# A graph layer in one launch: y rows read into three buffers, the end stage's first weights multiplied later, the first sums fetched at another place, and another order on VectorE in stage two

## Chip, cores and metric

The kernel is one program on one core of one Trainium2 chip. The metric is the device time of one execution in microseconds (us), lower is better, given as the median of several executions. Five engines run their own instruction lists: TensorE (PE in the profile, PEld for its weight loads), VectorE (DVE), ScalarE (ACT), GpSimd (POOL) and SyncE (SP). They meet only through semaphores that the program sets and waits for by hand.

## The reference, cut to what matters

All on 6250 rows of 512 numbers, in float32:

```python
xn = layernorm(x)                                    # 6250 x 512
h  = relu(xn @ W1 + b1) @ W2 + b2                    # a small network for each row
gnn = h + segment_sum(h[dst], src, 6250)             # 100000 edges: rows of h added up
k, q, v = split(layernorm(xn, g1, c1) @ kqv_w + kqv_b)
kp, qp = exp(k @ w.T - |k|^2/2) / 16, exp(q @ w.T - |q|^2/2) / 16
y = v + ((qp @ (v.T @ kp).T) / (qp @ sum(kp))) @ proj_w + proj_b
mix = y + gelu(layernorm(y, g2, c2) @ mlp_w1 + b) @ mlp_w2 + b2
x1 = x + gnn + mix
out = x1 + haar_ffn(layernorm(x1))                   # fc1, gelu and fc2 on the low-pass half
```

The fc1 of the last line acts on an interpolated row. The kernel folds the interpolation matrix and fc1 into one small matrix on the chip ("the end stage's first weights": `interp` times `fc1_t`).

## The kernel before, in words

The 6250 rows are 125 partitions times 50 tiles, and each of the 25 steps of a stage takes two tiles (250 rows, 500 KB). There are five stretches.

1. The start and **stage one** (up to about 450 us): weights are folded, keys and the hidden rows of the edge network are made, and the edges are sorted on VectorE.
2. **The turn** (to 512 us): small matrices between the stages.
3. **Stage two**, 25 turns (`phase2`, 512 to about 1026 us): TensorE makes v and the y product of step u and the q products of step u+1. The transposed x rows (`x_t`) come by DMA into `xt`, ScalarE copies their high halves (`high_parts`, L1300) and VectorE makes the low halves (`low_parts`, L1621); both halves are operands of step u+2. VectorE also squares (`square_sums`, L1745), makes exponents (`kqw_rows`, L1737), writes y rows (L2010), takes their statistics (`row_stats`, L1891) and so lets `store_y` write them to HBM.
4. **The mlp stage**, 25 turns (about 1026 to 1480 us). y rows and x rows come back by DMA: `load_yd` (L491) and `load_xd` (L513). ScalarE normalises y (`norm_rows`, L1397), TensorE transposes it (`transposes`, L980), makes the first layer (`features`, L1075 to L1077) and the second (`mlp2`, L1086 to L1088). VectorE adds x and y (`skip_rows`, L2051 and L2053) and then the second layer (`z_rows`, L2074), and SyncE stores z (`store_z`, L548). x and z share three buffers `z3`: x of step u+3 can be loaded only when z of step u has landed (`z_stored`). y rows have two buffers `y3`.
5. **The end stage** (to 1750 us): for the steps in another order, sums of the edges (`ACC`, fetched with `fetch_sums`, L529, transposed at L1110) meet z, and the fc1 and fc2 products follow.

From the turn on, all engines also work off 440 **groups** of edges: GpSimd gathers rows, ScalarE makes one-hot matrices (L1372, L1376: `one_hots`, four groups in a batch, made ahead by `hits_until`), TensorE multiplies (L942 to L945) into one of two banks, and VectorE adds the bank to `ACC` (L1871, `add_groups`). TensorE may be two groups ahead of VectorE's adds. How many groups stand at each place of a turn is fixed by the tables `SECOND`, `MLP` and `LAST`.

The order of everything on an engine is the order in which the program is written. All DMAs but the gathers are issued by SyncE, in its own order, on one queue. SyncE waits for each semaphore before it goes on, and an issue also waits while the queue is full. The part of SyncE's list between stage two and the mlp stage is, before the change:

```python
            sp.wait_ge(v_mm, STEPS + 1)
            load_yd(0, 1)
            load_xd(0)
            sp.dma_start(mlp2_w, chunks(d["L0_mix_mlp_w2"])).then_inc(w2m_in, 16)
            load_xd(1)
            load_xd(2)
            store_y(Step(2, STEPS - 1))
            sp.dma_start(gnn2_w, chunks(d["L0_gnn_W2"])).then_inc(late_in, 16)
            ...
            sp.dma_start(fc1_t, chunks(d["fc1_t"])).then_inc(ev_fc, 16)
            for a in range(STEPS):
```

and `late_io(a)` in the loop issues the loads and stores of turn a. "x of step u" and "y(u)" below are the 500 KB of that step. TensorE's order in mlp turn a is: features of step a, first half; groups; transposes of step a+1; mlp2 of step a-1, in two halves with groups between; features, second half; groups.

## Time and profile before

| | us |
|---|---|
| median of 3 runs | 1753.76 |
| lowest and highest run | 1750.54, 1756.96 |
| the profiled execution, own time | 1752.63 |
| its span in the profile | 1750.1 |
| TensorE busy | 1549.2 (89%) |
| GpSimd, VectorE, ScalarE busy | 1002.2, 1134.8, 820.4 |
| mean granted TensorE clock | 0.958 |

The span is the time from the first to the last instruction; 2.5 us of the execution's own time lie around it. A busy share says how full an engine is, not whether it is waited for; for that, one reads the idle pieces of the fullest engine, and what ended each. The granted clock is a share of TensorE's full 2.4 GHz; 0.50 is its other level, 1.2 GHz.

### The profile page before, as it was taken

Reading aid. Unit: us, or ns where it says so; the run is one execution under the profiler, and the core shown is the slowest. Engines: PE = TensorE matmul, PEld = TensorE weight load, DVE = VectorE, ACT = ScalarE, POOL = GpSimd, SP = SyncE. Lnnn points to the kernel's source line nnn. Section 1 sums busy time; section 2 is a strip of 40 time slices with the busy share of each in tenths; the row PEclk is TensorE's granted clock in tenths of the full one; section 3 lists DMA queues with packets and bytes.
Section 4 is the critical chain, followed back from the end, with each engine's and each line's share of the span. In section 5 each row is a group of like instructions: output and inputs, shape, how many; then the busy total and the mean of one; then the engine's idle time right before and its main releaser. Section 6 shows DMA issues by size and latency. Waiting matters only on the chain.

```text
span 1750.1 us, 26882 instructions
## 1 busy us (share of the span) xinstructions
PE 1549.2 (89%) x8883; PEld 1249.3 (71%) x8883; DVE 1134.8 (65%) x2523; ACT 820.4 (47%) x1896; POOL 1002.2 (57%) x1057
## 2 busy tenths in 40 slices
PE   5999999898888999998999976989898896689996
PEld 3778877787667778877778755877777775366664
DVE  6899999998245566545655553655565563478885
ACT  2235445454365434434534464566466462355552
POOL 3023443343677767775677776777777773456610
PEclk8999999999899999998999987999999998799997
DMA  6023222222345555655556565555555553566642
GB/s 195 13 78 122 86 92 89 89 89 72 119 121 166 185 159 168 180 171 152 169 168 185 160 195 165 196 189 191 189 194 189 193 182 108 154 206 211 204 161 73
DMA packets 88682, 263.63 MB, mean 151 GB/s; under 512 B 18555, under 2 KB 20603, under 8 KB 88546
## 3 DMA queue, kind: packets, MB, share of 16 engines
q1 hardware_dynamic: 47490, 149.05, 25.2%
q0 software_dynamic: 41056, 112.88, 22.3%
q8 instruction: 72, 1.18, 0.3%
q14 instruction: 64, 0.52, 0.1%
HBM read 210.64 MB, written 44.90 MB: 146 GB/s over the span
## 4 chain that ended last, share of the span: by engine, by line
PE 38%; DMA 24%; DVE 19%; ACT 7%; issue 6%; POOL 3%; SPq 2%; DVEq 1%; POOLq 0%; ACTq 0%
DVE sb_weights L1564 6%; DMA z_rows<-sb_step 5%; DMA sb_step<-x_t 4%; PE bank L1029 4%; DMA sb_step<-x 4%; DMA sb_step<-sb_acc 4%; PE bank L992 3%; PE bank L994 3%; PE bank L993 3%; DMA z_rows<-sb_weights 2%; ACT sb_weights L1372 2%; DMA sb_step<-y_rows 2%; DMA sb_weights<-x 2%; DVE sb_step L1745 2%; PE bank L943 1%
## 5 line engine op out<-in xcount | busy, mean ns | idle before, releaser
L679 POOL DMA_INDIRECT sb_weights<-hidden_rows,sb_weights x830 | 829.2, 999 | 366.5 <-issue 224.4
L1372 ACT ACTIVATE sb_weights<-sb_const,sb_weights 128x125 f16<-128x125 f16 x880 | 266.3, 389 | 41.4 <-PE turn_bank L945 41.4
L1871 DVE TENSOR_TENSOR sb_acc<-sb_acc,bank 125x257 f32 x220 | 92.4, 420 | 159.9 <-PE bank L945 144.3
L1871 DVE TENSOR_TENSOR sb_acc<-sb_acc,turn_bank 125x257 f32 x220 | 92.1, 419 | 120.7 <-PE turn_bank L945 110.9
L1564 DVE TENSOR_TENSOR sb_weights<-sb_weights 128x512 f32<-128x512 f32 (+3 forms) x256 | 164.4, 684 | 3.6
L1290 ACT ACTIVATE sb_step<-sb_step 125x256 f32<-125x256 f32 x100 | 48.9, 504 | 211.8 <-DVE sb_step L1737 211.1
L646 POOL TENSOR_SCALAR sb_const<-sb_const 125x2 f32<-125x2 f32 x25 | 10.1, 403 | 239.6 <-ACT sb_step L1274 239.6
L784 PE MATMUL bank<-sb_w_parts,sb_x_high 128*125 128x512 f32 (+1 forms) x400 | 140.0, 350 | 0.0
L785 PE MATMUL bank<-sb_w_parts,sb_x_high 128*125 128x512 f32 (+1 forms) x400 | 135.8, 339 | 0.0
L786 PE MATMUL bank<-sb_w_parts,sb_x_low 128*125 128x512 f32 (+1 forms) x400 | 135.7, 339 | 0.0
L1376 ACT ACTIVATE sb_weights<-sb_weights,sb_const 128x1000 f16<-128x1000 f16 x110 | 124.2, 1129 | 3.6
L1397 ACT ACTIVATE sb_step<-sb_step,sb_const 125x512 f32<-125x512 f32 x50 | 37.9, 805 | 175.6 <-DMA sb_step<-y_rows 173.7
L797 PE MATMUL bank<-sb_w_parts,sb_x_high 128*125 128x256 f32 (+1 forms) x300 | 102.9, 343 | 15.6 <-DVE sb_step L1745 12.9
L1411 ACT COPY sb_step<-bank 128x500 f32<-128x500 f32 x25 | 14.4, 577 | 210.1 <-PE bank L1014 210.1
L799 PE MATMUL bank<-sb_w_parts,sb_x_low 128*125 128x256 f32 (+1 forms) x300 | 94.8, 316 | 0.0
L798 PE MATMUL bank<-sb_w_parts,sb_x_high 128*125 128x256 f32 (+1 forms) x300 | 94.7, 316 | 0.0
L2065 DVE CAST sb_gelus_high<-sb_step 128x500 fp32r<-128x500 f32 x50 | 21.5, 429 | 112.9 <-ACT sb_step L1428 112.8
L1029 PE MATMUL bank<-sb_const,sb_step 128*125 128x512 f32 x200 | 93.9, 591 | 0.0
L897 PE MATMUL bank<-sb_step 125*128 125x256 f32 x400 | 90.8, 380 | 1.1 <-ACT sb_step L1350 1.1
L942 PE MATMUL bank<-sb_weights 128*125 128x257 f16 x220 | 62.2, 283 | 27.7 <-DVE sb_acc L1871 15.0
L1086 PE MATMUL bank<-sb_mlp_high,sb_gelus_high 128*125 128x512 f32 x200 | 85.0, 425 | 0.4 <-issue 0.4
L897 PEld LDWEIGHTS bank<-sb_step 125*128 125x128 f32 x400 | 75.3, 190 | 13.6 <-issue 2.9
(367 smaller groups left out, 4337.9 us busy)
## 6 DMA issues: line engine op xcount, KB each, us to landing
sb_step<-x SPq DMA_DIRECT2D x55, 500.0 KB
sb_step<-x_t SPq DMA_DIRECT2D x50, 500.0 KB, 6.1
sb_weights<-hidden_rows,sb_weights POOLq DMA_INDIRECT x830, 4.4
y_rows<-sb_step SPq DMA_DIRECT2D x25, 500.0 KB
sb_step<-y_rows SPq DMA_DIRECT2D x25, 500.0 KB
sb_weights<-x SPq DMA_DIRECT2D x20, 500.0 KB
z_rows<-sb_step SPq DMA_DIRECT2D x17, 500.0 KB
sb_step<-z_rows SPq DMA_DIRECT2D x13, 504.0 KB
```

Source lines behind the costliest of these rows:

```text
L679: pool.indirect_dma_start(out=ring[:, r % RING * 2 + h, 0:HID], out_offset=None, in_=table, in_offset=bass.IndirectOffsetOnAxis(ap=row_of[ ...
L784: pe.matmul(bk, high, rhs(0, c), start=c == 0, stop=False)
L785: pe.matmul(bk, high, rhs(1, c), start=False, stop=False)
L786: mm = pe.matmul(bk, low, rhs(0, c), start=False, stop=c == KC - 1)
L797: pe.matmul(outs[c], high, first, start=c == 0, stop=False)
L799: mm = pe.matmul(outs[c], low, first, start=False, stop=c == KC - 1)
L897: mm = pe.matmul((BC, BD)[k // 2][:, (k % 2) * M:(k % 2 + 1) * M], x_in[0:P, t.b, m, k * 128:(k + 1) * 128], kpn[0:P, m, :], start=False, ...
L1029: mm = pe.matmul(banks[m][0:P, :], qpT[:, c, m * P:(m + 1) * P], pmat[:, c, :], start=False, stop=c == KH - 1)
L1372: mm = act.activation(hit[q % 2][:, i, :], iota_h[:, :], ACT.Abs, bias=less_lane[:, q * BP + i // 2, i % 2:i % 2 + 1])
L1376: act.activation(hit[q % 2], hit[q % 2], ACT.Relu, scale=-1.0, bias=one_c[:, 0:1]).then_inc(hits, 1)
L1564: sort_op(dve.tensor_tensor(half(target, c, lo), a, b, op))
L1871: dve.tensor_tensor(dst, dst, (BE, BH)[n % 2][0:P, 0:RW], ALU.add).then_inc(g_add, 1)
```

## The change

Five edits, all in the order of work and in where rows lie; no arithmetic is added or removed.

- **y rows in three buffers.** `y3` gets a third place (`z_first[1]`), step u uses place u mod 3, and `late_io(a)` loads y(a+3) where it loaded y(a+2). y(0) is loaded in turn 23 of stage two (was: turn 11), and y(2) goes into the queue behind the `mlp2_w` load.
- **The end stage's first weights.** `fc1_t` gets a place in `mlp1_w`, is loaded in stage two's turn 12 (was: last of the loads between the stages), and `tail_weights` runs in mlp turn 2 (was: end of turn 0), in bank BB, with ScalarE's copy of its result moved along.
- **First sums.** The two `fetch_sums` move from turn 24 to turn 23, ahead of the store of z(22).
- **VectorE in stage two.** `low_parts(u+2)` moves from ahead of the squares of step u+1 to behind the y rows of step u. Squares and exponents are taken apart, with groups between.
- **VectorE in mlp turn 0.** `skip_rows(0)` moves behind `split_mlp2`.

```diff
-        y3 = [halves[1].rearrange("p (a b) -> p a b", b=D), y3_odd]
+        y3 = [halves[1].rearrange("p (a b) -> p a b", b=D), y3_odd, z_first[1]]
...
-        interp, fc1_t = (z4[h].rearrange("p a (b c) -> p (a b) c", c=HL) for h in (0, 1))
+        interp, fc1_t = (v.rearrange("p a (b c) -> p (a b) c", c=HL) for v in (z4[0], mlp1_w[:, 2:4, :]))
...
+            def load_yd(u):
+                sp.wait_ge(y_st[u % 2], 16 * (u // 2 + 1) + 1)
+                sp.dma_start(y3[u % 3][0:P], rows(y_d)[:, 2 * u:2 * u + 2, :]).then_inc(y_ld[u % 3], 16)
...
+                if t.u == STEPS - 2:
+                    sp.wait_ge(*made("mlp1_split"))
+                    load_yd(0)
...
-                elif t.u == 11:
-                    sp.wait_ge(r_st[0], 16 * 13 + 1)
-                    sp.wait_ge(r_st[1], 16 * 12 + 1)
+                elif t.u == 12:
                     sp.wait_ge(*made("mlp1_split"))
-                    load_yd(0, 0)
+                    sp.dma_start(fc1_t, chunks(d["fc1_t"])).then_inc(ev_fc, 16)
...
             def late_io(a):
-                if a + 2 < STEPS:
+                if a + 3 < STEPS:
                     sp.wait_ge(zadd, a + 2)
                     sp.wait_ge(h_rows, a + 2)
-                    load_yd(steps[a + 2].j, steps[a + 2].s)
+                    load_yd(a + 3)
                 if 2 <= a and a + 1 < STEPS:
                     z_stored(steps[a - 2])
                     load_xd(a + 1)
+                if a == STEPS - 2:
+                    fetch_sums(steps[0])
+                    fetch_sums(steps[1])
                 if a > 0:
                     store_z(steps[a - 1])
...
             sp.dma_start(mlp2_w, chunks(d["L0_mix_mlp_w2"])).then_inc(w2m_in, 16)
+            load_yd(2)
             load_xd(1)
...
-            sp.dma_start(fc1_t, chunks(d["fc1_t"])).then_inc(ev_fc, 16)
...
             def tail_weights():
 
                 pe.wait_ge(ev_fc, 33)
+                pe.wait_ge(feat_c, 2 * TAIL_TURN + 1)
...
-                        pe.wait_ge(ev("a_fc1"), 1)
                     pe.wait_ge(z_ok, a)
                     mlp2(steps[a - 1], 0)
+                if a == TAIL_TURN:
+                    tail_weights()
                 groups(counts[1])
...
-                add_groups(counts[0] + counts[1])
-                add_groups(counts[2] + counts[3] + counts[4])
-                if more:
-                    low_parts(Step(2, t.u + 2))
+                add_groups(counts[0] + counts[1] + counts[2] + counts[3])
                 if not last:
-                    q_rows(next_step(t))
+                    q_squares(next_step(t), 0)
+                add_groups(counts[4])
+                if not last:
+                    q_squares(next_step(t), 1)
                 add_groups(counts[5])
+                if not last:
+                    q_exponents(next_step(t))
...
                     add_groups(counts[6 + m])
+                if more:
+                    low_parts(Step(2, t.u + 2))
                 dve.wait_ge(y_read, t.u * 2 + 3)
...
+                if a > 0:
+                    skip_rows(steps[a])
...
                 if a == 0:
                     split_mlp2()
-                add_groups(counts[2])
+                    skip_rows(steps[a])
```

SyncE's list at the border of stage two and the mlp stage, after the last stores of y. L487 stores y, L491 loads y, L513 (L514 in the changed kernel) loads x, and `fc_t` at L581 is `fc1_t`. Before:

```order
L487 DMA y_rows<-sb_step 125x1024 x2
L491 DMA sb_step<-y_rows 125x1024
L513 DMA sb_step<-x 125x1024
L573 DMA sb_weights<-L_mix_mlp_w 128x4x512
L513 DMA sb_step<-x 125x1024
L513 DMA sb_weights<-x 125x1024
L487 DMA y_rows<-sb_step 125x1024
L577 DMA sb_weights<-L_gnn_W 128x2x512
L579 DMA sb_step<-fc_t 128x2x256
L580 DMA sb_weights<-c_interp 128x4x256
L581 DMA sb_weights<-fc_t 128x4x256
```

and now:

```order
L491 DMA sb_step<-y_rows 125x1024
L514 DMA sb_step<-x 125x1024
L577 DMA sb_weights<-L_mix_mlp_w 128x4x512
L491 DMA sb_weights<-y_rows 125x1024
L514 DMA sb_step<-x 125x1024
L514 DMA sb_weights<-x 125x1024
L487 DMA y_rows<-sb_step 125x1024
L582 DMA sb_weights<-L_gnn_W 128x2x512
L584 DMA sb_step<-fc_t 128x2x256
L585 DMA sb_weights<-c_interp 128x4x256
L491 DMA sb_step<-y_rows 125x1024 x2
```

The second y load (y(2)) now stands fourth, the last weight load is gone, and the two y loads at the end are y(3) and y(4), where y(2) and y(3) stood.

VectorE in the later part of a stage-two turn. L1621 makes the low halves of x_t for step u+2, L1745 squares, L1737 exponents, L1871 a group's add, L2010 a y row. Before, with the rows' numbers:

```order
1247 L1621 TENSOR_TENSOR sb_x_low<-sb_step,sb_x_high 128x1000
1248 L1745 SCALAR_TENSOR_TENSOR sb_step<-bank,sb_weights 125x512
1249 L1737 SCALAR_TENSOR_TENSOR sb_step<-bank,sb_const 125x256
1250 L1745 SCALAR_TENSOR_TENSOR sb_step<-turn_bank,sb_weights 125x512
1251 L1737 SCALAR_TENSOR_TENSOR sb_step<-bank,sb_const 125x256
1252 L1871 ISA
1253 L1871 TENSOR_TENSOR sb_acc<-sb_acc,turn_bank 125x257
1254 L2010 SCALAR_TENSOR_TENSOR sb_step<-bank,sb_const 125x512
```

and now, where the same instructions have lines L1624, L1748, L1740, L1874 and L2019:

```order
1227 L1748 SCALAR_TENSOR_TENSOR sb_step<-turn_bank,sb_weights 125x512
1228 L1874 ISA
1229 L1874 TENSOR_TENSOR sb_acc<-sb_acc,turn_bank 125x257
1230 L1740 SCALAR_TENSOR_TENSOR sb_step<-bank,sb_const 125x256 x2
1231 L2019 SCALAR_TENSOR_TENSOR sb_step<-bank,sb_const 125x512
1232 L1874 ISA
1233 L1874 TENSOR_TENSOR sb_acc<-sb_acc,bank 125x257
1234 L2019 SCALAR_TENSOR_TENSOR sb_step<-bank,sb_const 125x512
1235 L1874 ISA
1236 L1874 TENSOR_TENSOR sb_acc<-sb_acc,turn_bank 125x257
1237 L1624 TENSOR_TENSOR sb_x_low<-sb_step,sb_x_high 128x1000
```

The low halves have gone from ahead of the squares to behind both y rows; the statistics of the y rows, after which they are stored, come next.

TensorE where the end stage's first weights stood, at the end of mlp turn 0, before:

```order
L945 MATMUL turn_bank<-sb_weights 125x257
L1096 MATMUL bank<-sb_weights 128x256 x6
L1075 MATMUL bank<-sb_weights 128x250
L1076 MATMUL bank<-sb_weights 128x250
L1077 MATMUL bank<-sb_weights,sb_const 128x250
```

and now, in mlp turn 2 behind the first half of mlp2:

```order
L981 MATMUL turn_bank<-sb_const,sb_step 128x125 x4
L1087 MATMUL bank<-sb_mlp_high,sb_gelus_high 125x512
L1088 MATMUL bank<-sb_w_parts,sb_gelus_high 125x512
L1089 MATMUL bank<-sb_mlp_high,sb_gelus_low 125x512
...
L1098 MATMUL bank<-sb_step,sb_weights 128x256 x6
L943 MATMUL turn_bank<-sb_weights 125x257
```

The six products have moved over two turns, from ahead of step 1's features to behind the transposes of step 3 (L981) and half of mlp2 (L1087 to L1089).

## Rows read from the trace of the kernel before

**Rows 1.** Windows by stretch: us, busy of PE, PEld, DVE, ACT, POOL, PEclk, DMA share, GB/s.

```profile
512.00:1017.00 505.00, 483.48 (x2836) 391.48 (x2836) 285.79 (x797) 222.59 (x516) 355.00 (x359) 0.98 0.56 168
1017.00:1075.00 58.00, 29.69 (x192) 23.49 (x191) 19.12 (x37) 25.04 (x54) 43.16 (x43) 0.76 0.69 204
1075.00:1440.00 365.00, 332.24 (x2320) 280.34 (x2320) 212.37 (x366) 217.55 (x496) 266.39 (x267) 0.99 0.55 188
1440.00:1520.00 80.00, 50.26 (x251) 37.08 (x252) 25.10 (x56) 23.50 (x56) 32.98 (x35) 0.79 0.46 136
```

**Rows 2.** Waits of TensorE, whole span: us in total, times, longest.

```profile
PE bank L980 <- ACT sb_step L1397: 23.8, 20, 2.2
...
PE bank L1096 <- DMA sb_weights<-fc_t: 18.7, 1, 18.7
```

**Rows 3.** Stage two: waits of TensorE, then its timeline (start, us, work [idle before, releaser]).

```profile
PE turn_bank L942 <- DVE sb_acc L1871: 11.4, 4, 7.1
PE bank L942 <- ACT sb_weights L1376: 8.3, 6, 3.1
PE bank L942 <- DVE sb_acc L1871: 1.9, 2, 1.5
...
746.02 0.32 PE L942 MATMUL bank<-sb_weights 128*125 128x257 f16 x1 [1.41 <-ACT sb_weights L1376]
...
793.28 0.45 PE L942 MATMUL turn_bank<-sb_weights 128*125 128x257 f16 x1 [7.11 <-DVE sb_acc L1871]
```

**Rows 4.** The chain that ended last, stage two: start, us, what.

```profile
773.31 15.09 DMA sb_step<-x_t
...
820.95 7.37 DMA sb_step<-x_t
```

**Rows 5.** Timeline of VectorE, stage two.

```profile
789.47 1.20 DVE L1621 TENSOR_TENSOR sb_x_low<-sb_step,sb_x_high 128x1000 fp32r<-128x1000 f32 x1 [8.47 <-ACT sb_x_high L1300]
```

**Rows 6.** Windows behind stalls of TensorE, columns as in rows 1.

```profile
584.00:588.00 4.00, 4.00 (x13) 3.02 (x13) 3.67 (x16) 2.30 (x6) 2.96 (x4) 0.59 0.39 110
792.00:800.00 8.00, 6.72 (x20) 5.47 (x21) 6.57 (x23) 5.29 (x12) 1.91 (x2) 0.57 0.24 71
...
1458.00:1461.00 3.00, 2.94 (x9) 2.54 (x10) 0.68 (x1) 0.58 (x1) 0.00 (x0) 0.50 0.14 55
```

**Rows 7.** The chain that ended last, between the stages, and SyncE's queue 1014 to 1072.

```profile
1054.29 17.57 DMA sb_step<-y_rows
q1 hardware_dynamic: 2999, 6.31, 35.3%
```

**Rows 8.** Timeline of TensorE, first mlp turns.

```profile
1038.20 0.45 PE L942 MATMUL bank<-sb_weights 128*125 128x257 f16 x1 [6.55 <-DVE sb_acc L1871]
1064.54 4.81 PE L1096 MATMUL bank<-sb_weights 128*128 128x256 f32 x12 [18.71 <-DMA sb_weights<-fc_t]
```

**Rows 9.** Timeline of ScalarE, norm rows of step 3.

```profile
1083.49 1.50 ACT L1397 ACTIVATE sb_step<-sb_step,sb_const 125x512 f32<-125x512 f32 x2
```

**Rows 10.** Timeline of VectorE, skip rows of steps 1, 2 and 5.

```profile
1075.72 1.22 DVE L2051 TENSOR_TENSOR sb_step<-sb_step 125x1024 f32<-125x1024 f32 x1
...
1089.16 1.22 DVE L2051 TENSOR_TENSOR sb_weights<-sb_weights,sb_step 125x1024 f32<-125x1024 f32 x1
...
1140.12 1.23 DVE L2051 TENSOR_TENSOR sb_weights<-sb_weights,sb_step 125x1024 f32<-125x1024 f32 x1 [2.13 <-DMA sb_weights<-x]
```

**Rows 11.** The chain that ended last, a stretch of the mlp stage.

```profile
1247.06 13.54 DMA z_rows<-sb_step
1260.62 11.65 DMA sb_step<-x
...
1279.51 14.15 DMA z_rows<-sb_step
```

**Rows 12.** The first sums: the chain that ended last, then TensorE's timeline.

```profile
1444.65 13.28 DMA sb_step<-sb_acc
1458.06 1.07 PE L1110 MATMUL bank<-sb_const,sb_step 125*128 125x125 f32 x4 [10.75 <-DMA sb_step<-sb_acc]
```

More of the change, by code:

```diff
@@ L500, in _ @@
                 if t.u == 1:
-                    sp.wait_ge(ev("pe_pmat"), 1)
+                    sp.wait_ge(*made("pmat_product"))
                     sp.dma_start(mlp1_w, chunks(d["L0_mix_mlp_w1"])).then_inc(w1_in, 16)
@@ L906, in _ @@
                 mm = pe.matmul(bk[:, :], zero_row[0:1, 0:128], zero_row[0:1, :].unsqueeze(1).to_broadcast([1, 2, M]), start=False, stop=True)
-            mm.then_inc(ev("pe_hk"), 1)
+            mm.then_inc(made("hk_sums")[0], 1)
             pe.wait_ge(kadd, STEPS + 1)
@@ L911, in _ @@
                 mm = pe.matmul(BF[:, 0:M], ones[0:P, :], kps[0:P, m, :], start=m == 0, stop=m == 1)
-            mm.then_inc(ev("pe_ksum"), 1)
+            mm.then_inc(made("k_sums")[0], 1)
             def q_product(t, m):
@@ L956, in mlp_bias @@
                                        start=k == 0, stop=k == KC - 1)
-                mm.then_inc(ev("pe_mbias"), 1)
+                mm.then_inc(made("mlp_bias")[0], 1)
             def mlp1_norms():
@@ L1047, in _ @@
                 mm = pe.matmul(bk, bv_bc[0:1, c * 128:(c + 1) * 128], ks_bc[0:1, :], start=False, stop=True)
-            mm.then_inc(ev("pe_kptv"), 1)
+            mm.then_inc(made("kptv_product")[0], 1)
             groups(TURN[0])
@@ L1060, in _ @@
                                    start=c == 0, stop=c == KC - 1)
-            mm.then_inc(ev("pe_pmat"), 1)
+            mm.then_inc(made("pmat_product")[0], 1)
             groups(TURN[2])
@@ L1391, in norm_rows @@
             def norm_rows(t):
[L1392 removed]
+                act.wait_ge(y_ld[t.u % 3], t.u // 3 * 16 + 17)
                 act.wait_ge(tr, t.g * 2 + 1)
@@ L1875, in _ @@
             dve.memset(ring_h[:, :, ONE], 1.0).then_inc(ones_in, 1)
-            dve.wait_ge(ev("pe_ksum"), 1)
-            dve.wait_ge(ev("pe_hk"), 1)
+            dve.wait_ge(*made("k_sums"))
+            dve.wait_ge(*made("hk_sums"))
             for i, bk in ((0, BC), (1, BD)):
@@ L1900, in _, with q_squares, q_exponents @@
             own2 = Chain(dve_own[1], 10)
-            def q_rows(t):
+            def q_squares(t, m):
+                if m == 0:
+                    dve.wait_ge(x2_ld[t.b], 16 * (t.u // 2 + 1) + 1)
+                square_sums(t, m, (BA, BG)[m], x2[t.b])
+            def q_exponents(t):
                 for m in (0, 1):
-                    if m == 0:
-                        dve.wait_ge(x2_ld[t.b], 16 * (t.u // 2 + 1) + 1)
-                    square_sums(t, m, (BA, BG)[m], x2[t.b])
                     kqw_rows(t, m, BB[0:P, m * M:(m + 1) * M], bqw_bc, 2)
-            dve.wait_ge(ev("pe_kptv"), 1)
+            dve.wait_ge(*made("kptv_product"))
             for i, bk in ((0, BC), (1, BD)):
@@ L1912, in _ @@
             add_groups(TURN[0])
-            q_rows(Step(2, 0))
+            for m in (0, 1):
+                q_squares(Step(2, 0), m)
+            q_exponents(Step(2, 0))
             add_groups(TURN[1])
-            dve.wait_ge(ev("pe_pmat"), 1)
+            dve.wait_ge(*made("pmat_product"))
             for m, bk in ((0, BC), (1, BD)):
@@ L1929, in mlp_gains @@
             def mlp_gains():
-                dve.wait_ge(ev("pe_mbias"), 1)
+                dve.wait_ge(*made("mlp_bias"))
                 dve.tensor_tensor(m1b[:, :], m1b[:, :], BF[:, 0:KC], ALU.add)
@@ L2049, in skip_rows @@
                 dve.wait_ge(x3_ld[t.u % 3], t.u // 3 * 16 + 17)
-                dve.wait_ge(y_ld[t.s], t.j * 16 + 17)
-                dve.tensor_tensor(z, z, y3[t.s][0:P], ALU.add).then_inc(zadd, 1)
+                dve.wait_ge(y_ld[t.u % 3], t.u // 3 * 16 + 17)
+                dve.tensor_tensor(z, z, y3[t.u % 3][0:P], ALU.add).then_inc(zadd, 1)
                 dve.wait_ge(zadd, t.u + 2)
@@ L2143, in _ @@
                 add_groups(counts[0])
-                skip_rows(steps[a])
+                if a > 0:
+                    skip_rows(steps[a])
                 if a + 1 < STEPS:
```

36 lines of the change are left out of this document (15 added, 21 removed).

## The prediction

> **What bounds the kernel now.** I read the windows by stretch first. TensorE is the fullest engine everywhere, and the reader is to see how much of each stretch it stands still: 21.5 us of 505 in stage two, 28.3 of 58 between the stages (at a granted clock of 0.76), 32.8 of 365 in the mlp stage and 29.7 of 80 at its end (0.79) [rows 1]. Then the waits of TensorE: 18.7 us in one piece for `fc1_t`, 23.8 us in 20 pieces for norm rows that themselves wait for y [rows 2], and in stage two 13.3 us for VectorE's adds and 8.3 us for one-hots [rows 3]. Last the chain that ended last, which tells which of these waits set the pace. In the mlp stage it is not y: it runs z store 13.5, x load 11.7, 7.2 us of VectorE (skip rows, low halves, adds, z rows), z store again [rows 11]. That lap spans two turns, 1279.51 - 1247.06 = 32.45 us, 16.2 a turn. TensorE has 332 us of work for some 22.3 turns, 14.9 a turn [rows 1], and turn 2, whose x was there early, took 1089.16 - 1075.72 = 13.4 us [rows 10]. So the stage is paced by transfers, with TensorE 1.3 to 2.8 us a turn below.
>
> **Stage two: VectorE's order.** Of the 13.3 us, the large piece is 7.1 us at 793 [rows 3]. There the load of y(0) stood ahead of x_t in the queue, which took 15.1 us instead of 7.4 [rows 4]; `low_parts` waited 8.5 us [rows 5] with the squares and a group's add behind it, and TensorE waited for the add. In the new order the adds don't stand behind x_t until the end of the turn, so I take 12.8 us of the 13.3 as gone. Behind the stalls TensorE ran at its lower level: 4.0 us at 0.59 and 6.7 busy us at 0.57 [rows 6], which costs 1.6 + 2.9 = 4.5 us. Gain 17.3.
>
> What it costs: `low_parts` (1.2 us [rows 5]) now stands ahead of the statistics that release the store of y, and that store goes into the queue some 3 us ahead of the next x_t. So x_t lands up to 1.2 us later, and ScalarE's `high_parts` and the one-hots behind it too. One-hots are already short in each fourth turn (1.4 us at 746, 0.6 at 987 [rows 3]): a batch is four groups, a turn has seven, and in turns 6, 10, 14, 18 and 22 the batch made behind `high_parts` is used in the same turn. 5 x 1.2 = 6 us. `fc1_t` takes the place of y(0) in the queue, one turn later: x_t(15) is then late by about the same 15.1 - 7.4 = 7.7 us. Its turn needs no batch made behind it, but VectorE waits at the turn's end, y is stored some 3 us late and the next x_t with it, in turn 14, one of the five: 3 us. Net gain of stage two 17 - 9 = 8 us. Bounds: 0 (every turn pays 0.7 us for the later store) to 17 (slack takes it all).
>
> **Between the stages.** Today: 6.6 us of wait for VectorE's skip rows of step 0, 18.7 for `fc1_t`, 4.8 of product, nearly all at the lower level [rows 8], then y(2), landing at 1054.29 + 17.57 = 1071.9 [rows 7]. Three things change. `skip_rows(0)` no longer holds adds and low halves, so turn 0 goes on where it stood for 6.6 us, and ends when VectorE has split the mlp2 weights (nothing is put ahead of them in the queue) and then added x and y: an estimate of 1045. y(2) is behind the last store of stage two, y(1), x(0) and the 1 MB of mlp2's weights, with itself 3.1 MB from about 1014 on, which at the rate below is 28 us: 1043. Turn 1 starts at 1045 and not after 1069. But now y(3) is the last of the long list. The queue moved 6.31 MB in 58 us, 109 GB/s [rows 7], so 0.5 MB is 4.7 us; the list is shorter by `fc1_t`, and y(3) lands at 1071.9 - 4.7 = 1067 where y(2) did. TensorE would be ready for it at about 1062. So part of the stall stays, one turn later. Norm rows of step 3 began at 1083.5 [rows 9]: 16 us gained there. The product itself, 4.8 us mostly at the lower level, is 2.5 at full clock, inside turn 2 with its wait on gelus of step 1, which ScalarE does just after y(3). From there the turns run at TensorE's 14.2 (the middle of 13.4 and 14.9) until the lap of z and x takes over: z(0) is stored at 1058 behind a full queue and lands near 1077, x(3) near 1087; z(1), stored at 1081, brings x(4) at about 1103; x(5) comes at about 1120, where it was 1140.1 [rows 10]. Gain 20 us at step 5, and the rest of the stage hangs on that. Bounds: 12 (y(3) lands with y(2)'s time and z(0) is a further service late) to 26 (no stall left in turn 2).
>
> **The mlp turns.** The 23.8 us of waits for norm rows go, but y is loaded at the same point of the turn, so the queue carries the same three 0.5 MB pieces in the same order, and the lap of z and x is as long as before. TensorE's stall moves to VectorE's add behind `skip_rows`. Only laps in which y was the later one gain, about one. I take 2 us. Bounds: 0 to 22 turns x 1.3 = 29 (turns of 14.9).
>
> **The first sums.** They are issued at 1444.65, behind the store of z(22), land after 13.3 us, and TensorE stands 10.8 us [rows 12]. In the new order they go ahead of z(22) (4.7 us less) and behind x(24) at once (2 to 3 us earlier), and the last y load is gone from turn 22, so that z(21), and x(24) with it, is some 5 us earlier. Together 12 us, more than the 10.8. The cover of the wait is the features and the group of turn 24. The 3 us at 0.50 behind it [rows 6] give back 1.5, and the last two turns, free of y loads, about 1. Gain 13. Bounds: 7 (only the place ahead of z(22) and the earlier issue) to 15. Nothing waits behind the moved fetches but the store of z(22), which VectorE hands over at about the same time.
>
> **The sum.** 8 + 20 + 2 + 13 = 43 us. The profiled execution took 1752.6 (span 1750.1 and 2.5 around it): 1709.6. The median of the runs is 1.1 higher: 1710.7, rounded to 1711.
>
> The Trainium skill, DMA: Bandwidth & Descriptors, section "Anatomy of one DMA", fits a transfer as 2.0 us plus bytes at 436 GB/s. By it a 0.5 MB piece is an estimated 3.2 us, and z and x together 6.4 where the rows have 25 [rows 11]; the trace does not agree, and with such transfers the mlp turn would be TensorE's own.
>
> **Rivals.**
> - *Turns at TensorE's pace.* If the load on the queue, and not its bytes, makes the 13.5 and 11.7 us, the same edits bring turns of 14.9: 25 us more, about 1683. For it: between the stages the queue moved 109 GB/s, while three 0.512 MB pieces in 16.2 us are only 95 [rows 7, 11]. Against it: the order and time of issues in a turn stay, and each piece already waits for the one before.
> - *The stalls stay and only change names.* y(3) lands no earlier than y(2) did, so between the stages only 12 come back; stage two pays what it gains (0), the sums give 8: 20 us, about 1733. For it: the queue is full from 1014 to 1072 with any order [rows 7].
> - *Slower.* In stage two, `low_parts` now stands ahead of y's statistics. If x_t lands after VectorE reaches it, y is stored later, and the next x_t, behind that store, is later again. It lands 7.4 us after issue [rows 4], I work out about 3 us before VectorE gets there. If the lap closed, each of 24 turns would lose; from 1.8 us a turn it eats the whole 43, at 2.5 the time is 1753 + 60 - 43 = 1770. Against it: a single late x_t runs out within two turns by the sum above.
> - *No change*: the same lap at 1.8 us a turn, about 1753.
>
> **Chances.** Forecast (1695 to 1724) 0.60; stalls that change names (1724 to 1745) 0.18; turns at TensorE's pace (below 1695) 0.14; no change 0.04; slower 0.04. The forecast with the near half of both neighbours gives 1688 to 1733 for 8 in 10. Within 0.3% (5 us) of before a measurement can't tell a change: faster 0.92, same 0.04, slower 0.04.
>
> **What would show it.** Right: no wait of TensorE for `fc1_t`; a wait for norm rows only once, in turn 2, of about 5 us; skip rows of step 5 some 28 us earlier on the clock of the span (20 and stage two's 8); in the middle of the mlp stage turns of 16.2 us with z store and x load in the chain; the sums at L1110's new line without a wait. In stage two the waits for adds gone and those for one-hots up from 8.3 to about 17. Wrong: turns below 15.5 us (then the lap was not fixed), L1621's new line waiting turn after turn (the slower rival), or a wait for y(3) above 10 us.

## The result and the profile after

The changed kernel took 1738.4 us (median of 4 runs, 1735.3 to 1745.3) against 1755.4 us for the kernel before timed beside it: a ratio of 0.990, 95% interval 0.988 to 0.993. A second series (e11) gave 0.986, 0.984 to 0.989. So the change makes the kernel faster, by 17 to 24 us (the two ratios times the time before); forecast were 43. The profiled execution of after is the longest of its four (1745.3 us, span 1743.0), 7 us above their median; where it matters, the profile of e11 stands beside it, a second series of the changed kernel (1731.9 us, profiled execution 1731.7).

The windows of the changed kernel, in the columns of [rows 1]:

```profile
512.00:1014.00 502.00, 483.72 (x2837) 391.56 (x2836) 287.17 (x797) 221.53 (x515) 355.99 (x360) 0.99 0.57 170
1014.00:1075.00 61.00, 39.32 (x272) 31.75 (x270) 27.94 (x51) 32.85 (x73) 46.68 (x48) 0.89 0.68 203
1075.00:1440.00 365.00, 329.53 (x2260) 281.31 (x2261) 205.84 (x357) 213.15 (x477) 264.28 (x264) 0.95 0.55 186
1440.00:1520.00 80.00, 57.93 (x282) 41.82 (x281) 31.53 (x73) 25.57 (x61) 37.65 (x40) 0.83 0.47 142
```

Between the stages TensorE is busy 39.3 us of 61 where it was 29.7 of 58; in the mlp stage it is not fuller than before. There its granted clock is 0.95 (0.97 in e11) where it was 0.99: its waits there are longer, up to 14.9 and 6.1 us against 2.2. The prediction had no term for that, and no run here prices it. Its waits in the three stretches (stage two, then 1014 to 1440, then 1440 to 1460; total, times, longest):

```profile
PE bank L943 <- ACT sb_weights L1379: 16.7, 8, 4.0
PE turn_bank L943 <- DVE sb_acc L1874: 1.6, 2, 1.3
...
PE turn_bank L943 <- DVE sb_acc L1874: 35.8, 19, 6.1
PE bank L981 <- ACT sb_step L1400: 14.9, 1, 14.9
...
PE bank L1112 <- DMA sb_step<-sb_acc: 5.0, 1, 5.0
```

In stage two the adds' 13.3 us [rows 3] are 1.6, and the one-hots' 8.3 are 16.7. The 23.8 us for norm rows [rows 2] have become one wait of 14.9 in turn 2 (12.6 in e11), and TensorE waits 35.8 for the adds behind the skip rows in their place. The sums' 10.8 us [rows 12] are 5.0.

What happened to y(3) and z(0), from the timeline of SyncE (start, length of the issue), and what ScalarE waited for in turn 2 (both of after):

```profile
1053.29 9.34 SPq L491 DMA_DIRECT2D sb_step<-y_rows  x2
1062.69 1.48 SPq L549 DMA_DIRECT2D z_rows<-sb_step  x1
1081.82 0.25 SPq L491 DMA_DIRECT2D sb_weights<-y_rows  x1
1087.99 0.26 SPq L514 DMA_DIRECT2D sb_step<-x  x1
```

```profile
1076.54 1.52 ACT L1400 ACTIVATE sb_step<-sb_step,sb_const 125x512 f32<-125x512 f32 x2 [21.59 <-DMA sb_step<-y_rows]
```

y(3), issued at 1053.3, landed at 1076.5, not at 1067. z(0) was issued at 1062.7 behind it and y(4), and had landed only at 1088.0, when the load of x(3), which waits for that, was issued. SyncE's queue from 1014 to 1072, beside the 6.31 MB of [rows 7] (packets, MB, share of 16 engines):

```profile
q1 hardware_dynamic: 2529, 6.01, 33.6%
```

The lap in the mlp stage is still z store, x load and VectorE, as in [rows 11], and no shorter (the chain that ended last, after):

```profile
1144.31 15.02 DMA z_rows<-sb_step
1159.35 11.80 DMA sb_step<-x
1171.17 1.24 DVE sb_step L2062
```

Where the gain arises, from two pairs of profiles: the first ones of before and after, and e12 and e11, the same two kernels profiled again on one chip. The marks are ScalarE's last copy of `qpT` in stage two, skip rows of step 5 and of step 24, and the end of the span, each in us from the span's start:

```
                        stage two's end   step 5   step 24   span
before                           1016.9   1140.1    1449.7   1750.1
after                            1013.5   1136.0    1446.2   1743.0
e12, before again                1021.6   1145.8    1454.7   1757.3
e11, after again                 1010.9   1126.1    1433.9   1729.9
```

So the stretches gave, in the first pair and in the second: stage two 3.4 and 10.7 us (forecast 8), from there to step 5 0.7 and 9.0 (forecast 20), from step 5 to 24 -0.6 and 1.1 (forecast 2), and behind that 3.6 and 6.6 (forecast 13).

### The profile page after: what moved, and what is told of

Its sections match the earlier page's. It is cut to its first block, busy times and chain, and to the rows that moved or that the text cites. A ratio compares the mean times of both kernels' runs of the same rounds, so it can differ in the third digit from the quotient of the medians.

```text
span 1743.0 us, 26881 instructions
## 1 busy us (share of the span) xinstructions
PE 1555.3 (89%) x8883; PEld 1256.4 (72%) x8883; DVE 1135.4 (65%) x2523; ACT 821.2 (47%) x1896; POOL 1001.7 (57%) x1057
## 4 chain that ended last, share of the span: by engine, by line
PE 39%; DMA 25%; DVE 17%; ACT 7%; issue 6%; POOL 3%; SPq 1%; DVEq 1%; POOLq 0%; ACTq 0%
DMA sb_step<-x 7%; DMA z_rows<-sb_step 7%; DVE sb_weights L1567 6%; PE bank L1030 4%; DMA sb_step<-sb_acc 3%; DMA sb_step<-x_t 3%; ACT sb_weights L1375 3%; PE bank L993 3%; PE bank L995 3%; PE bank L994 3%; DMA z_rows<-sb_weights 2%; PE bank L785 1%; PE bank L786 1%; PE bank L787 1%; PE bank L944 1%
## 5 line engine op out<-in xcount | busy, mean ns | idle before, releaser
L1874 DVE TENSOR_TENSOR sb_acc<-sb_acc,bank 125x257 f32 x220 | 92.8, 422 | 206.6 <-PE bank L946 187.0
L1874 DVE TENSOR_TENSOR sb_acc<-sb_acc,turn_bank 125x257 f32 x220 | 92.4, 420 | 113.3 <-PE turn_bank L946 103.7
L1431 ACT ACTIVATE sb_step<-bank,sb_const 128x250 f32<-128x250 f32 x100 | 50.5, 555 | 158.3 <-PE bank L1078 107.4
L943 PE MATMUL turn_bank<-sb_weights 128*125 128x257 f16 x220 | 61.2, 278 | 37.4 <-DVE sb_acc L1874 37.4
L1076 PE MATMUL bank<-sb_weights 128*128 128x250 f16 x300 | 86.3, 288 | 0.0
L1077 PE MATMUL bank<-sb_weights 128*128 128x250 f16 x300 | 85.6, 285 | 0.0
```

The lines of the kernel that those rows point to most:

```text
L943: pe.matmul(bk[0:P, 0:RW], one_hot, row[:, LOW_AND_ONE], start=True, stop=False)
L1874: dve.tensor_tensor(dst, dst, (BE, BH)[n % 2][0:P, 0:RW], ALU.add).then_inc(g_add, 1)
```

## The experiments

Ratios are to the kernel before, timed beside it on the same chip, with their 95% interval. To read them: the changed kernel is 0.990 and 0.986 in its two series, with intervals from 0.984 to 0.993, so a ratio inside these bounds is called no measurable difference from it. The pace is (skip rows of step 22 less those of step 4) / 18, from VectorE's timeline of each: 16.51 us a turn before, 16.54 after.

### Seven runs on the order and place of transfers

**e1, VectorE's order in stage two alone**, on the kernel before:

```
-    add_groups(counts[0] + counts[1])
-    add_groups(counts[2] + counts[3] + counts[4])
-    if more: low_parts(Step(2, t.u + 2))
-    if not last: q_rows(next_step(t))
-    add_groups(counts[5])
+    add_groups(counts[0] + counts[1] + counts[2] + counts[3])
+    q_squares(next_step(t), 0); add_groups(counts[4]); q_squares(next_step(t), 1)
+    add_groups(counts[5]); q_exponents(next_step(t))
...
+    if more: low_parts(Step(2, t.u + 2))          (behind the y rows)
```

> The kernel before with VectorE's order in stage two alone. By the prediction's sum this term is 17 less 6 us, so 11 faster, about 1744 (its 3 us for fc1_t do not arise; the load of y(0) stays in turn 11). By my reading of the trace of the changed kernel (stage two ends 3.3 us earlier, one-hot waits 8.3 -> 16.7 us) it is 3 to 6 faster, about 1751. Rival: the gain is given back later, since the queue works off the same list after stage two: no change, 1755.

Measured: 0.994 (0.992 to 0.996), 1750.1 us; 9 us by the medians of that series. In its trace one-hots wait 17.9 us in stage two and the adds 1.6, but stage two ends where it did in the first profile of before (1016.9), and the span is the same (1750.6 and 1750.1). Against the second profile of before (e12) stage two ends 4.7 us earlier and the span is 6.7 shorter. The timing says faster; profiles that differ this much from one execution to the next can't say where.

**e7, first sums back where they were**, the rest as changed:

```
-                if a == STEPS - 2:
-                    fetch_sums(steps[0]); fetch_sums(steps[1])
+    (ahead of late_io(a) for a == STEPS - 1)
```

> The changed kernel with the first two fetches of sums put back where they stood, ahead of turn 24's z store. My prediction's term is 13 us for the move, of which about 1 is from the y loads; so 12 slower than the changed kernel, 1750. By the trace of the changed kernel the wait went from 10.8 to 5.0 us, and the end stage gave some of it back: 4 to 6 slower, 1743.

Measured: 0.990 (0.987 to 0.992), 1741.4 us. L1112 waits 10.2 us where the changed kernel has 5.0. The time of the whole kernel can't tell the two apart, but the end stage can: from skip rows of step 24 to the end of the span e7 takes 303.9 us, the changed kernel 296.8 and 296.0, and before and e12 300.4 and 302.6. So the move is worth 4 to 8 us behind step 24, and nothing near 13.

**e8, exponents ahead of the adds, `low_parts` behind y's statistics**, in stage two of the changed kernel:

```
+                if not last: q_exponents(next_step(t))
                 add_groups(counts[5])
-                if not last: q_exponents(next_step(t))
...
                 row_stats(...).then_inc(y_ok[t.s], 1)
+                if more: low_parts(Step(2, t.u + 2))
```

> The changed kernel with two orders of VectorE in stage two moved again: exponents of the next step ahead of the adds of the sixth count, low_parts behind the statistics that release the store of y. Theory 1 (the one-hot waits grew to 16.7 us because ScalarE's exponentials, and the one-hots behind them, start later, and because y is stored later): one-hot waits fall to 8 to 11 us, stage two ends 4 to 6 us earlier, and the time falls by 0 to 5, as the queue takes over behind stage two. Rival: the waits come from x_t alone (the two of 4 us are behind it): they stay within 2 us of 16.7, no change.

Measured: 0.986 (0.983 to 0.990), 1738.8 us. One-hot waits fall to 12.2 us (8 to 11 were expected) and ScalarE's last qpT copy of stage two is at 1007.7 (1013.5 and 1010.9 in the two profiles of the changed kernel). Step 24 starts at 1441.4, inside what the changed kernel shows (1433.9 and 1446.2). Stage two's 3 to 6 us are given back by step 5 (1128.8, against 1126.1 and 1136.0), in line with theory 1.

**e2, 1.3 MB out of the list between the stages**:

```
-            sp.dma_start(gnn2_w, ...); sp.dma_start(fc2_w, ...); sp.dma_start(interp, ...)
+                if a == 5: gnn2_w  elif a == 6: fc2_w  elif a == 7: interp      (in late_io)
-TAIL_TURN = 2, late_weights in turn 3
+TAIL_TURN = 10, late_weights in turn 9
```

> The changed kernel with 1.3 MB (gnn2_w, fc2_w, interp) taken out of the queue between the stages and issued in mlp turns 5, 6 and 7, the tail product in turn 10, late_weights in turn 9. Theory 1 (the opening's list is what holds z(0) and so x(3), x(4); the mlp turns have room in the queue): z(0) lands about 12 us earlier than 1088, step 5 starts about 10 us earlier than 1121, turns 6 to 9 lose about 3 of it again: 5 to 10 us faster than the changed kernel, about 1730. Theory 2 (the queue is saturated through the mlp stage as well, bytes moved are only moved): the three pieces cost in turns 5 to 7 what they gave before, 1738.

Measured: 0.987 (0.984 to 0.991), 1731.6 us. Skip rows of step 5 start at 1116.3, which is 10 to 20 us ahead of the changed kernel (1126.1, 1136.0); steps 6 to 9 then start 18.3 to 19.8 us apart, and no measurable time is left. The tail product's move to turn 10 is part of this run and wasn't tried by itself.

**e3, x and z in four buffers**, on e2:

```
-        z3 = [x3[:, 0], x3[:, 1], z_first[2]]
+        z3 = [x3[:, 0], x3[:, 1], z_first[2], z_first[0]]
-                    load_xd(a + 1)
+                    load_xd(a + 2)        (% 4 and // 4 wherever % 3 and // 3 stood for x and z)
```

> As the kernel with the short list, and x and z rows in four buffers instead of three, so that the store of z, the load of x and VectorE's rows of one step may take three turns and not two. Theory 1 (the mlp turns of 16.4 us are a lap of latencies in a queue that is not saturated): turns fall to TensorE's 14.9, some 20 turns x 1.5 = 30 us, about 1700. Theory 2 (the queue moves 1.5 MB a turn at its full rate): turns stay at 16.2 or more, z store and x load become longer than 14 and 11 us, 1730 to 1738.

Measured: 0.989 (0.986 to 0.992), 1735.9 us, and the pace is 17.0 us a turn. SyncE's timeline of e3:

```profile
1324.98 0.26 SPq L515 DMA_DIRECT2D sb_weights<-x  x1
1325.29 0.34 SPq L550 DMA_DIRECT2D z_rows<-sb_weights  x1
1325.74 0.28 SPq L492 DMA_DIRECT2D sb_weights<-y_rows  x1
1341.36 0.26 SPq L515 DMA_DIRECT2D sb_weights<-x  x1
```

x, z and y are issued together and the next three 16.4 us later, when z has landed; its store alone takes 16 us now. A third more room for the lap gave nothing, so the lap isn't one of fixed latencies: each piece takes longer to land when more of them stand in the queue. Three pieces in 16.4 us are 5.5 us each.

**e4, store of z(0) ahead of the load of y(4)**: `if a == 1: store_z(steps[0])` ahead of `load_yd(a + 3)`.

> The changed kernel with the store of z(0) issued ahead of the load of y(4). Theory 1: z(0) lands one piece, 5 us or a little more, earlier, x(3) and x(4) with it, and the whole stage: 1733. y(4) lands 5 us later, for norm rows of step 4, which have slack of some 10 us. Theory 2: the saturated queue gives y(4) back what z(0) got, steps 4 and 5 start where they did: 1738.

Measured: 0.986 (0.984 to 0.989), 1737.6 us: the changed kernel's time. Step 5 starts at 1130.8, between the changed kernel's two profiles.

**e5, y in ScalarE's queue**, on e2:

```
-                    load_yd(a + 3)                                  (SyncE, late_io)
+                    act.dma_start(y3[a % 3][0:P], rows(y_d)[:, 2 * a + 6:2 * a + 8, :]).then_inc(y_ld[a % 3], 16)
```

> As the kernel with the short list (e2), with the loads of y(3) to y(24) issued by ScalarE into its own queue at the end of its part of a turn, instead of by SyncE in the middle of it. So far the turns of e2 and e3 stand at 16.2 to 16.4 us with three 0.5 MB pieces each, 5.4 us a piece. Theory A (the limit is SyncE's one queue, which works off its pieces one after another): with two pieces a turn it needs 11 us, turns fall to TensorE's 14.9, z stores to 10 us, total about 1700. Theory B (the limit is what the transfers and the gathers together may move, about 190 GB/s, whichever queue they stand in): turns stay at 16.2, time 1732 as e2.

Measured: 0.987 (0.985 to 0.989), 1736.7 us, pace 17.1 us (with e2's three pieces in it). The DMA view of e5, 1200 to 1400 (queue: packets, MB, share of 16 engines), q10 being ScalarE's:

```profile
q1 hardware_dynamic: 3088, 12.16, 15.6%
q10 hardware_dynamic: 1560, 6.14, 8.3%
```

Two queues together move 18.3 MB in 200 us; the one of the changed kernel 18.6. So the limit isn't SyncE's queue. The Trainium skill, DMA: Bandwidth & Descriptors, section "Issuing engines are not separate DMA queues", says that DMAs run on the same 16 engines whichever engine starts them; the unchanged 18.3 MB agree with it.

### What a piece of 125 rows runs on

**e6, half of each y piece** from step 4 on, on e2. The second half of each y buffer keeps old rows, so norm and skip rows of every second tile are computed from other data.

> As e2, but from step 4 on only the first half of each y piece (0.25 of 0.5 MB) is loaded; the second half of the buffer keeps old rows, so skip rows and norm rows of the second half compute with other data. Both theories of a full queue: 2.5 pieces a turn, 13.5 us of queue, so turns fall to 14.9, 20 x 1.4 = 28 us faster than e2, about 1704. Rival (lap of fixed latencies, the bytes don't matter): turns stay at 16.2, 1732.

Measured: 0.967 (0.965 to 0.969), 1700.8 us, pace 15.3 us. So the bytes count: 0.25 MB less a turn is worth 31 us against e2.

What the bytes wait for I counted from the packets in the traces: how many packets of SyncE's queue (e5: and ScalarE's) are under way, at points 50 ns apart from 1189.5 to 1339.5 us of the span, and the median time of a packet. A packet here is one row of a piece, 4096 bytes for both tiles of a step; in e14, which comes below, it is 2048.

```
kernel                  none   1 to 5   6 or more   packet
before                    1%      95%          4%   162 ns
after                     1%      95%          3%   162 ns
e5, both queues           2%      94%          4%   161 ns
e14, two narrow parts     2%      87%         10%    84 ns   (2048 bytes)
e9,  wide                50%      10%         39%   195 ns
e15, wide, five groups   44%      12%         44%   199 ns
after, 1011.5 to 1019.5   0%      42%         58%   170 ns   (weights of 128 rows among them)
```

The queue is hardly ever idle in the mlp stage (1 to 2% of the time), but it seldom has more than five packets under way, though the core has 16 DMA engines and their mean busy share is 0.55. The pieces have 125 rows. The Trainium skill, DMA: Bandwidth & Descriptors, section "Why a DMA increments its semaphore by 16 and not by 1", says that a DMA is spread over the largest number of engines up to 16 that divides the slowest dimension of both sides. By this rule 125 rows use 5. The counts agree; which engine a packet ran on, the traces don't show. The prediction did without it.

**e9, x, y and z pieces of the mlp stage in two parts, of 112 and 13 rows**, on the changed kernel:

```
+            def both(out, in_, done):
+                for part in (slice(0, 112), slice(112, P)):
+                    sp.dma_start(out[part], in_[part]).then_inc(done, 16)
-                sp.dma_start(y3[u % 3][0:P], ...).then_inc(y_ld[u % 3], 16)
+                both(y3[u % 3][0:P], ..., y_ld[u % 3])                (waits count 32 a piece; x and z alike)
```

> The changed kernel with each load of x and y and each store of z in the mlp stage issued as two, rows 0 to 111 and rows 112 to 124, instead of one of 125 rows. So far: a piece takes 5.4 us of the queue whether in SyncE's queue or with y in ScalarE's (e5), and half a y piece gives the turn back 1.2 us (e6). In the trace of the changed kernel between 1200 and 1400 us no more than five packets of SyncE's queue are under way at once (90% of the time), while 128-row weights had up to 16. Theory E (a piece of 125 rows runs on five of the 16 DMA engines, and these are the bound): turns fall from 16.4 to TensorE's 14.9, z stores from 14.7 to under 8 us, about 30 us faster than the changed kernel, 1710. Theory B (the sum of all transfers, 190 GB/s, is the bound, whatever carries them): no change, 1742.

Measured: 0.970 (0.968 to 0.971), 1705.2 us, pace 15.6 us. **e14, two parts again, but each of 125 rows and half the columns**:

```
+                for part in (slice(0, 1), slice(1, 2)):
+                    sp.dma_start(out[:, part], in_[:, part]).then_inc(done, 16)
```

> The changed kernel with each mlp-stage piece as two of 125 rows and half the columns (0.25 MB each), so as many issues as in e9, but each still on five engines. Theory E: turns stay at 16.4 to 16.6, 1732 to 1742 as the changed kernel. If splitting alone helps (more pieces under way, shorter ones): turns at 15.6 as in e9, 1705.

Measured: 0.991 (0.989 to 0.994), 1741.8 us, pace 16.9 us. As many issues as e9, and again seldom more than five packets under way: no gain. Its packets are half as large, but a packet takes 84 ns where it took 162, so their size costs little. That tells the number of parts from the number of engines: it is the engines.

**e10, every 125-row piece of all stages in two parts**, on e9 (x rows, r rows, x2 rows, y stores, stores of out).

> As the kernel before this one, with all other 125-row pieces split too: x rows, r rows, x2 rows and y stores of stages one and two, and the stores of out in the end stage. Theory E: x_t in stage two lands earlier (7.4 -> 5 us), the one-hot waits behind it fall from 16.7 to about 10, the opening shortens, the end stage's waits for z and sums as well: another 10 us or more, about 1698. Theory B: 1742.

Measured: 0.958 (0.957 to 0.960), 1685.8 us, 20 us below e9, but the pace is 16.1 us. The waits of TensorE in e10, 1120 to 1400, and GpSimd's gathers there (line, count | busy us, mean ns | idle before, of it issue):

```profile
PE turn_bank L947 <- DMA sb_weights<-hidden_rows,sb_weights: 22.3, 15, 2.1
```

```profile
L684 POOL DMA_INDIRECT sb_weights<-hidden_rows,sb_weights x211 | 216.0, 1024 | 64.3 <-issue 59.4 <-PE turn_bank L950 4.3 <-PE bank L950 0.6
```

TensorE now waits for gathers (apart from 0.5 us), and GpSimd issues 211 of them back to back, with 4.9 us of waiting in 280: 275.4 / 211 = 1.31 us each, 12 a turn are 15.7 us, for a turn of 16.1. The changed kernel shows how near this limit was before (the same view):

```profile
L680 POOL DMA_INDIRECT sb_weights<-hidden_rows,sb_weights x203 | 202.8, 999 | 78.7 <-issue 54.9 <-PE bank L946 14.1 <-PE turn_bank L946 9.7
```

202.8 + 54.9 us for 203 gathers are 1.27 each, 15.2 a turn of 16.5. GpSimd was 92% taken, though its busy share, as in [rows 1] for before, 266 of 365 us, shows 73%.

### Both limits

**e11 and e12, the two kernels again**, for a profile of each from one chip.

> The changed kernel itself, for its time and a profile of the same chip as the two experiments beside it. Ratio 0.990, about 1742; step 5's skip rows between 1127 and 1136.

> The kernel before itself, for a second profile: how far its stages move from one execution to the next. Ratio 1.000, step 5's skip rows at 1140 within 3.

Measured: e11 0.986 (0.984 to 0.989), 1731.9 us; e12 0.998 (0.996 to 1.000), 1754.0 us. Profiles of one kernel differ: step 5's skip rows at 1126.1 (e11) and 1136.0 (the first profile of after), at 1145.8 (e12) and 1140.1 (before). From e12 to e11: `qpT`'s last copy 10.7 us earlier, step 5's skip rows 19.7, step 24's 20.8, the end of the span 27.4. So most of the gain is made by step 5, the mlp turns add next to nothing, and the end stage adds 6.6.

**e13, the kernel before with all pieces in two parts.**

> The kernel before with every 125-row piece split as in e10. If the five engines hid the change's gain (theory E), the change is worth more here: the kernel before falls by less than the changed one did (46 us), to about 1725, and the difference to e10 (1686) is about 40 us, near the 43 that I had predicted for the change. If the change's own steps are small whatever carries the pieces: 1708, 22 us above e10.

Measured: 0.957 (0.954 to 0.959), 1677.2 us, against 0.958 (0.957 to 0.960) for e10. On wide pieces the change is worth nothing. My expectation, that the five engines hid its gain, is wrong the other way round: there is a gain only while the pieces are narrow. In stage two the waits of TensorE from 512 to 1010, e13 first, then e10:

```profile
PE bank L946 <- ACT sb_weights L1380: 2.9, 2, 1.5
PE turn_bank L946 <- DVE sb_acc L1875: 2.1, 4, 1.1
```

```profile
PE bank L947 <- ACT sb_weights L1383: 8.4, 5, 3.2
PE turn_bank L947 <- DVE sb_acc L1878: 2.0, 3, 1.4
```

With wide pieces x_t, 128 rows itself but queued among them, lands 4.2 us after its issue (the median, 7.1 before), and VectorE stands still ahead of `low_parts` for 3.7 us in stage two where it stood 22.9. With x_t in time the old order has few adds to wait for, and the new one still has its one-hots. e13 ends stage two at 995.0 (qpT's last copy), e10 at 1002.8.

**e16, e10 with the edits of e4 and e8.**

> As e10 with the store of z(0) ahead of the load of y(4) and the exponents of stage two ahead of the adds (e4 and e8 on wide pieces). Both gave nothing measurable where the queue took it back. With the queue no longer the limit stage two's 4 us should reach the end: 1682. Rival: GpSimd's gathers are the floor of stage two and of the mlp turns, and take it back as the queue did: 1686.

Measured: 0.956 (0.954 to 0.959), 1680.8 us. Its interval overlaps e10's, so it is undecided.

**e15, five groups instead of six in mlp turns 1 to 24**, on e10: `[10] + [6] * (STEPS - 1)` becomes `[10] + [5] * (STEPS - 1)`. The same one edit makes **e17** from the changed kernel, and **e18** from e13.

> As e10 with five groups instead of six in each of the mlp turns 1 to 24; the 24 groups go to the end stage. GpSimd issues a gather each 1.27 us or more, 12 a turn: 15.3 us at least, 16.0 as the trace of e10 has it (211 gathers in 280 us with 5 us of waiting). Theory G (this issue is the floor of the turn): 10 gathers are 13.3, turns fall to TensorE's 14.2 (14.9 less a group's 0.9), 24 x 1.8 = 43 us less there, and the end stage takes on 24 groups x 0.9 = 22 us of TensorE and 48 gathers where GpSimd is busy half the time: 10 to 20 faster than e10, about 1671. Theory B (190 GB/s in sum): the turn falls to 2.83 MB / 190 GB/s = 14.9, so much the same here; the two differ in the gathers' waits, which stay under B and go under G. No gain (1686) if the end stage is bound by the groups.

> The changed kernel, its 125-row pieces as they are, with five groups instead of six in mlp turns 1 to 24. If the five engines are a limit of their own (three pieces at 5.2 to 5.4 us): turns stay at 15.6 to 16.2, 24 x 0.6 = 14 us less there and 22 us of groups more in the end stage, partly in its waits: 1725 to 1745. If GpSimd was the only limit of the narrow turn: turns of 13.8 as in e15, about 1700.

> The kernel before with split pieces (e13) and five groups in mlp turns 1 to 24: turns of 13.8 as in e15, 31 us less than e13: 1646. If the change helps once both limits are gone, it stays above e15's 1655; if its order of VectorE in stage two costs, as the one-hot waits of e10 (8.4 us against 2.9 in e13) say, it comes out below.

Measured: e15 0.941 (0.938 to 0.943), 1654.8 us; e17 0.989 (0.986 to 0.992), 1736.8 us; e18 0.943 (0.940 to 0.945), 1656.4 us. The window of e15, its longest wait of TensorE, and the two of e17, 1120 to 1400 each (the sums' 8.0 us stand at the end of the stage):

```profile
1120.00:1400.00 280.00, 266.41 (x1865) 229.20 (x1863) 169.82 (x284) 161.04 (x360) 197.33 (x199) 0.99 0.71 199
```

```profile
PE bank L1116 <- DMA sb_step<-sb_acc: 8.0, 1, 8.0
```

```profile
PE turn_bank L943 <- DVE sb_acc L1874: 13.4, 15, 1.5
PE bank L943 <- DVE sb_acc L1874: 11.1, 14, 1.3
```

The four cells, pace of a turn and ratio:

```
                      six groups (12 gathers)   five groups (10 gathers)
narrow pieces (5)     16.6 us  0.986 (e11)      15.7 us  0.989 (e17)
wide pieces (16)      16.1 us  0.958 (e10)      13.8 us  0.941 (e15)
```

With one of the two limits taken away the turn is still 15.6 to 16.1 us (e9, e10, e17); only without both is it TensorE's own, 13.79 us turn after turn, with 199 GB/s moved, so no sum of 190 GB/s was the limit either. e18 shows the same for the old order: pace 13.79, and a ratio that can't be told from e15's, so the change is worth nothing there either.

The two limits aren't independent. With narrow pieces, too, two gathers less a turn made it 0.9 us shorter. From 1200 to 1340 us the gathers' queue takes 31.0% of the 16 engines' time in the changed kernel and SyncE's 23.9%; in e17 it is 28.1% and 25.2%. If the gathers fall evenly on all engines, and the pieces on five, the packets on these five add up to an estimated 5 x 0.310 + 16 x 0.239 = 5.4 engines' time in the one and 5 x 0.281 + 16 x 0.252 = 5.4 in the other: five full engines both times, shared with the gathers. That is argued, not shown, since the traces don't name a packet's engine.

Why e17 takes no less time, the marks show: skip rows of step 24 start at 1418.2 (1433.9 in e11), and from there to the end it takes 316.6 us where e11 takes 296.0. The 24 groups cost 20.6 us in the end stage, 0.86 each, and that eats the 15.7 won before. On wide pieces the end stage pays less for them: 298.3 in e15 and 284.8 in e10, 13.5 us.

## Why the prediction was wrong, point by point

The sign and most of the waits were as forecast: no wait for `fc1_t`, one wait for norm rows in turn 2, the mlp stall renamed to the adds, z store and x load in the chain, one-hots up to 17 us. The time was outside the range in both series, since two terms were far too large.

- **Between the stages, 20 us: the step that failed.** "The list is shorter by `fc1_t`, and y(3) lands at 1071.9 - 4.7 = 1067." But y(2) is new in that list, as large as `fc1_t`, so the bytes ahead of y(3) are as many as there were ahead of y(2). They also drain more slowly: `fc1_t` has 128 rows and y(2) 125, and from 1014 to 1072 the queue moved 6.01 MB (5.79 in e11) where it had moved 6.31. y(3) landed at 1076.5 (1068.8 in e11). Counted from the end of stage two that is 63.0 and 57.9 us, where y(2) took 55.0 and 55.4 in the two profiles of before and the forecast made it 50.3. TensorE waited 14.9 us (12.6 in e11) and not 5, which the prediction itself names as a sign of being wrong. With it the next number fell: z(0), expected to land at 1077, landed at 1088.0 (1079.3 in e11), since it stood behind y(3) and y(4) (0.5 MB each). That y(4) is now issued ahead of z(0) I hadn't counted at all. In the first pair of profiles step 5 is 4.1 us earlier, in the pair e12 and e11 19.7, forecast were 28. e2 showed that the list is what holds the opening; in e4 the 5 us of one place in it don't show. Of the 20 us, 9 are there in the pair e12 and e11 (19.7 less stage two's 10.7), about 1 in the first.
- **Stage two, 8 us: right in mechanism, size uncertain.** Waits 13.3 to 1.6 and 8.3 to 16.7 as written; the end of the stage moved by 3.4 us in the first pair and 10.7 in the second; e1 alone measured 9 us. What I had not seen is that the late x_t is itself the five engines' doing: with wide pieces stage two ends at 1002.8 in the new order and at 995.0 in the old.
- **mlp turns, 2 us: right.** The pace stayed (16.51, 16.54). The reason given, a lap of z and x through a queue, was half of it. The piece's 5.4 us are those of five engines, and GpSimd's 15.2 us a turn stand close behind. My floor of 14.9 for TensorE (rival "turns at TensorE's pace") was not reached by another order or queue: e3 (17.0) and e5 (17.1) tried, and e9, which lifts the first limit, stopped at 15.6, with TensorE waiting 17.5 us for gathers between 1120 and 1400.
- **First sums, 13 us: mis-sized.** The wait went from 10.8 to 5.0, so 5 to 6, and the stretch behind step 24 is 4 to 7 us shorter; undone in e7, it is 7 to 8 longer. I had x(24) and z(21) 5 us earlier because y loads had gone. That didn't come: x(24) was issued at 1437.9 (1441.4 before), 3.5 us earlier as all of step 24 was, the sums behind it at 1439.2, and they landed 10.2 us later.
- **The rivals.** "The stalls stay and only change names" (20 us, 1733) is the one that the time and the renamed waits bear out, though not term by term: it had 12 us between the stages and none in stage two, where 1 to 9 and 3 to 11 were measured. The chance of 0.18 was too low; the row that speaks for it, a queue full from 1014 to 1072, was read but given little weight. "Slower" did not happen: x_t was in time, and VectorE stood still ahead of `low_parts` not once in stage two, where before it stood 22.9 us in 13 turns.

The fit of 2.0 us and 436 GB/s that the prediction takes from the Trainium skill (DMA: Bandwidth & Descriptors, section "Anatomy of one DMA") is given in that section for transfers that GpSimd issues; the pieces compared with it are SyncE's and use five engines. The sum of the prediction doesn't use it.

What stays open: where in the kernel e1's 9 us lie, why two profiles of one kernel differ by 3 to 10 us at the end of stage two and at step 5, and what TensorE's lower clock in the mlp stage costs.

## What to carry to other kernels

Before moving transfers about, find out why one piece takes as long as it does. Here 0.5 MB took 5.4 us of the queue, and the number of engines that 125 rows divide into was most of the answer: splitting every piece into 112 and 13 rows, without touching the order of anything, gave 4.3% on the kernel before (e13), and with one group fewer in each mlp turn 5.7% (e18), against 1.0 to 1.4% for the change. When moving transfers, count the bytes ahead of each piece that somebody waits for; a piece that leaves a list and one that takes its place cancel. And take as the floor of a turn the fullest engine with its issue time, not its busy share: GpSimd showed 73% and was at 92%.

## What the hardware showed unexpectedly

DMAs of 125 rows kept to five packets at a time (about 95% of the time, 3 to 4% more than five) at 162 ns for 4096 bytes, also when spread over two queues (e5); cut by columns (e14) they were at 87% and 10%, with 84 ns for 2048 bytes. Cut into 112 and 13 rows, the packets took 195 ns each, with the queue idle half of the time. GpSimd took 1.27 us for each gather (203 of them from 1120 to 1400), 1.0 of it shown as busy and 0.3 as issue. And two profiles of the changed kernel, from two series, differ by 10 us at step 5 of the mlp stage (1126.1 and 1136.0), which is more than most of the reorderings here moved.
